# An order of its own for the first two images of a group-norm and attention kernel

## The reference

```python
g = group_norm(x, 32 groups, eps=1e-5)            # mean and variance over 6 channels x 1024 positions
qkv = einsum('bnc,oc->bno', g_tokens, qkv_w)      # 6 heads of 32
attn = softmax(einsum('bhnd,bhmd->bhnm', q, k) * 32**-0.5)
out = einsum('bhnm,bhmd->bhnd', attn, v)          # 1024 x 1024 per head
y = x + (out @ proj_w.T + proj_b)
```

## Time and profile before

| | us |
|---|---|
| median of 3 runs | 1629.27 |
| lowest, highest | 1627.18, 1630.30 |
| profiled execution, time | 1626.17 |
| profiled execution, span | 1624.4 |
| PE busy | 1502.3 (92%) |
| POOL busy | 1319.5 (81%) |
| ACT busy | 1197.5 (74%) |
| DVE busy | 1164.1 (72%) |

### The profile page before, as it was taken

One profiled execution on the slowest core, in us unless ns is written; L12 is line 12 of the kernel. 1 busy time (PEld: TensorE's weight loads), 2 busy tenths in 40 slices (PEclk: granted clock), 3 DMA queues, 4 the chain that ended last, 5 costly groups with the idle time before them and its releaser, 6 DMA issues.

```text
span 1624.4 us, 24488 instructions
## 1 busy us (share of the span) xinstructions
PE 1502.3 (92%) x8800; PEld 514.2 (32%) x8800; DVE 1164.1 (72%) x2022; ACT 1197.5 (74%) x2001; POOL 1319.5 (81%) x645
## 2 busy tenths in 40 slices
PE   3379999999999999999999999999999999999872
PEld 1123233333333333333333333333333333333210
DVE  3387868778787877877786877877787887877500
ACT  2138787877869787887978787887968787777750
POOL 4028898988989898998989898998989898888880
PEclk9989999999999999999999999999999999999985
DMA  2304051352616043251515144251615223141112
GB/s 73 59 27 86 22 94 39 78 88 54 106 41 116 24 103 57 63 102 54 105 41 105 28 94 72 57 108 35 117 37 100 45 76 64 54 86 37 30 46 59
DMA packets 86105, 108.86 MB, mean 67 GB/s; under 512 B 38240, under 2 KB 50912, under 8 KB 85984
## 3 DMA queue, kind: packets, MB, share of 16 engines
q1 hardware_dynamic: 85984, 107.30, 32.2%
HBM read 42.98 MB, written 13.15 MB: 35 GB/s over the span
## 4 chain that ended last, share of the span: by engine, by line
PE 62%; DMA 9%; ACT 8%; POOL 5%; SPq 5%; issue 2%; DVE 2%; POOLq 0%; DVEq 0%; ACTq 0%
PE heads_ps L561 16%; PE max_ps L470 14%; PE scores_ps L546 14%; DMA sums_spread<-sums_sb 7%; PE extra_ps L520 6%; ACT probs L675 4%; PE extra_ps L529 3%; SPq L351 3%; POOL prob_pairs L728 2%; POOL prob_pairs L734 2%; PE extra_ps L533 2%; PE extra_ps L531 2%; PE extra_ps L530 2%; PE extra_ps L534 2%; SPq L428 1%
## 5 line engine op out<-in xcount | busy, mean ns | idle before, releaser
L675 ACT ACTIVATE probs<-scores_ps,exp_scale 128x512 f32<-128x512 f32 x1536 | 974.8, 698 | 292.5 <-PE scores_ps L546 287.2
L829 DVE TENSOR_REDUCE half_max<-max_ps 128x1 f32<-128x512 f32 x1536 | 981.1, 682 | 290.2 <-PE max_ps L470 279.9
L728 POOL TENSOR_TENSOR prob_pairs<-probs 128x1024 f32<-128x1024 f32 x384 | 896.3, 2360 | 173.9 <-ACT probs L675 173.2
L470 PE MATMUL max_ps<-k_stack,q_stack 96*128 96x512 f16 x1536 | 588.1, 384 | 23.9 <-DVE half_max L829 14.8
L546 PE MATMUL scores_ps<-q_stack,k_stack 98*128 98x512 f16 x1536 | 581.7, 380 | 14.0 <-DMA q_stack<-shift_rows 8.1
L561 PE MATMUL heads_ps<-probs,v_sb 128*32 128x512 f32 x3072 | 410.7, 607 | 1.5 <-ACT probs L675 0.8
L470 PEld LDWEIGHTS max_ps<-k_stack,q_stack 96*128 96x128 f16 x1536 | 150.3, 98 | 297.5 <-issue 104.2
L734 POOL TENSOR_TENSOR prob_pairs<-prob_pairs 128x1024 f32<-128x1024 f32 x96 | 224.2, 2357 | 0.0
L546 PEld LDWEIGHTS scores_ps<-q_stack,k_stack 98*128 98x128 f16 x1536 | 150.2, 98 | 182.2 <-ACT probs L675 34.1
L520 PE MATMUL extra_ps<-prob_pairs,ones 128*32 128x512 f32 x1152 | 134.0, 598 | 5.8 <-POOL prob_pairs L728 5.8
L561 PEld LDWEIGHTS heads_ps<-probs,v_sb 128*32 128x32 f32 x3072 | 61.0, 108 | 152.4 <-issue 130.5
(11 more groups left out here) (82 smaller groups left out, 956.8 us busy)
## 6 DMA issues: line engine op xcount, KB each, us to landing
q_stack<-qk_hi SPq DMA_DIRECT2D x96, 128.0 KB, 4.2
k_stack<-qk_hi SPq DMA_DIRECT2D x96, 128.0 KB, 5.8
inv_sb<-inv_rows SPq DMA_DIRECT2D x48, 256.0 KB
x_res<-x SPq DMA_DIRECT2D x16, 768.0 KB, 5.4
out<-x_res SPq DMA_DIRECT2D x16, 768.0 KB, 4.8
x_sb<-x SPq DMA_DIRECT2D x16, 512.0 KB, 6.7
x_sb<-x SPq DMA_DIRECT2D x32, 256.0 KB, 8.0
q_stack<-qk_lo SPq DMA_DIRECT2D x48, 128.0 KB, 4.5
```

What stands on the lines that cost most here:

```text
L470: pe.matmul(max_ps[:, bank, :], q_stack[0:STACK, par, h, P * tile:P * (tile + 1)], k_stack[0:STACK, par, h, HALF * half:HALF * (half + 1)] ...
L675: nc.scalar.activation(probs[:, a, s % RING, HALF * half:HALF * (half + 1)], scores_ps[:, u_bank(s, u), :], ACT.Exp, scale=exp_scale[:, 0: ...
L728: nc.gpsimd.tensor_tensor(prob_pairs[:, a, q, :], probs[:, a, (s - 1) % RING, :], probs[:, a, s % RING, :], ALU.add).then_inc(pairs_added, 1)
L829: nc.vector.tensor_reduce(half_max[:, a, tile, half:half + 1], max_ps[:, bank, :], AX_X, ALU.max).then_inc(max_read[bank], 1)
```

## The change

It gives steps -2 and -1 their own lists of slots, and changes these things:

- The six qk products of image 0 go to six banks (`qk_bank`: extra_ps, heads_ps, the three scores banks, one max bank), and PE no longer waits for `extra_freed` between them. All later products go through extra_ps as before.
- SP stacks pair 0 of image 0 once four products are read, pair 1 and pair 2 once all six are; image 1's norm is written between pairs 0 and 1 and read between pairs 1 and 2.
- There are two x buffers (and two of `chan_norm`). Image 1 is loaded right behind the constants, image 2 in step -2 at slot 10, image 3 in step -1 at slot 23; from step 0 on, image b+4 at slot 10.
- Statistics of image 1 are taken by DVE during the weights' setup and aggregated behind it; its POOL operations come in slot 11 of step -2. From step -1 on, bn_stats of image b+3 stand in slots 8 to 11, one a slot, instead of two each in slots 16 and 17.
- In step -1 the value products are in slots 10, 13, 14, 15 (14, 15, 18, 20 before), the qk products of image 1 in 19, 21, 22 (17, 19, 22), the shift of pair 0 in slot 20 (21), ACT's normalisation of image 1 in slots 16 to 19 (3 to 9), POOL's low parts in 18 and 20 (8 and 10).
- In the last attending step the shifts are in slots 4 and 12 (5 and 13), whose move stands in SP's program before the heads' moves of slots 5 and 13.

```diff
-STATS_AT = ((16, 1), (16, 3), (17, 1), (17, 3))
+STATS_AT = ((8, 1), (9, 1), (10, 1), (11, 1))
...
-QK_SECOND_SLOTS = (17, 19, 22)
-V_SECOND_SLOTS = (14, 15, 18, 20)
+QK_SECOND_SLOTS = (19, 21, 22)
+V_SECOND_SLOTS = (10, 13, 14, 15)
+SHIFT_FIRST_SLOTS = {20: 0}
+SHIFT_LAST_SLOTS = {4: 1, 12: 2}
+XHAT_SECOND_AT = ((16, 1), (16, 3), (17, 1), (17, 3), (18, 1), (18, 3), (19, 1), (19, 3))
+XLO_SECOND_SLOTS = (18, 20)
+RSTD_SECOND_SLOT = 11
+STACK_FIRST_SLOTS = {16: 0, 18: 1, 20: 2}
+NORM_SECOND_SLOTS = (17, 19)
+LOAD_SECOND_SLOT = 23
...
-        self.take_stats = 0 <= at + 3 < BATCH
+        self.take_stats = -1 <= at < BATCH - 3
+        self.first, self.second = at == -2, at == -1
...
+        self.shift_slots = {-1: SHIFT_FIRST_SLOTS, BATCH - 1: SHIFT_LAST_SLOTS}.get(at, SHIFT_SLOTS)
...
-        x_sb = sb("x_sb", [P, 2, N], F32)
+        x_sb = sb("x_sb", [P, 2, 2, N], F32)
...
+        def qk_bank(st, i):
+
+            if not st.first or i == 0:
+                return extra_ps[:, :]
+            return heads_ps[:, :] if i == 1 else (scores_ps[:, i - 2, :] if i < 5 else max_ps[:, 0, :])
...
+            load_x(1)
...
+            write_stats(0)
+            read_stats(0)
+            write_norm(0)
+            write_stats(1)
+            read_norm(0)
+            read_stats(1)
...
+                    if st.first and s in STACK_FIRST_SLOTS:
 
                         sp.wait_ge(extra_freed, st.ordinal(s))
-                        for p in range(PAIRS):
-                            stack_pair(st.parity, p)
+                        stack_pair(st.parity, STACK_FIRST_SLOTS[s])
+                    if st.first and s == NORM_SECOND_SLOTS[0]:
+                        write_norm(1)
+                    if st.first and s == NORM_SECOND_SLOTS[1]:
+                        read_norm(1)
...
-                    if s == LOAD_SLOT and st.project_in and b + 3 < BATCH:
+                    if s == st.load_slot and -2 <= b < BATCH - 4:
                         sp.wait_ge(xhat_ready, XHAT * (b + 3))
-                        load_x(b + 3)
+                        load_x(b + 4)
...
-                if part == 0 and due(g):
+                if part == 0 and due(g) and not st.first:
                     pe.wait_ge(extra_freed, g)
...
-            statistics(-3)
+            statistics(0)
+            for n in range(2 * HALVES):
+                half_statistics(1, n)
             dve.wait_ge(l1_ready, 1)
...
+            statistics(1)
```

More of the change, by code:

```diff
@@ L127, in __init__ @@
         self.late = at >= 0 and self.follow
+        self.shift_slots = {-1: SHIFT_FIRST_SLOTS, BATCH - 1: SHIFT_LAST_SLOTS}.get(at, SHIFT_SLOTS)
+        self.xhat_at = XHAT_SECOND_AT if self.second else XHAT_AT
+        self.xlo_slots = XLO_SECOND_SLOTS if self.second else XLO_SLOTS
+        self.load_slot = LOAD_SECOND_SLOT if self.second else LOAD_SLOT
         self.extras = extras
     def extra(self, s):
-        if s in SHIFT_SLOTS and (self.follow if SHIFT_SLOTS[s] == 0 else self.attend):
-            return "shift", SHIFT_SLOTS[s]
+        if s in self.shift_slots and (self.follow if self.shift_slots[s] == 0 else self.attend):
+            return "shift", self.shift_slots[s]
         if self.follow and s in self.v_slots:
@@ L284, in group_norm_attention @@
         shift_set = sem("shift_set")
-        x_loaded = sem("x_loaded")
+        x_loaded = [sem(f"x_loaded{i}") for i in range(2)]
         stats_step = sem("stats_step")
@@ L356, in step @@
                 for s in range(SLOTS):
[L357 to L367, removed]
@@ L379, in step @@
-                    if s == QK_FIRST_SLOTS[-1] + 1 and not st.follow and st.project_in:
-                        sp.wait_ge(extra_freed, st.ordinal(s))
-                        for p in range(PAIRS):
-                            stack_pair(st.parity, p)
+                    if st.project_in and st.attend and s == NORM_OUT_SLOT:
+                        write_norm(b + 2)
+                    if st.project_in and st.attend and s == NORM_IN_SLOT:
+                        read_norm(b + 2)
+                    if st.take_stats and s == STATS_OUT_SLOT:
+                        write_stats(b + 3)
@@ L491, in fill @@
                     o, n = slice(P * t, P * (t + 1)), slice(HALF * half, HALF * (half + 1))
-                    last = product(part, extra_ps[:, :], w_hi[:, :, o], w_lo[:, :, o], xhat_a_hi[:, par, n],
+                    last = product(part, qk_bank(st, i), w_hi[:, :, o], w_lo[:, :, o], xhat_a_hi[:, par, n],
                                    xhat_a_lo[:, par, n], xhat_b[:, par, n])
@@ L872, in step @@
                             read(st, s - 1)
[L873 to L876 removed]
+                        if st.take_stats and (s, u) in STATS_AT:
+                            half_statistics(st.b + 3, STATS_AT.index((s, u)))
+                        if st.take_stats and (s, u) == AGGREGATE_AT:
+                            statistics(st.b + 3)
                         if st.maxed(s) is not None:
```

109 lines of the change are left out of this document (66 added, 43 removed).

## The result

| | before | after |
|---|---|---|
| median, us | 1629.00 (4 runs) | 1588.78 (4 runs) |
| lowest, highest | 1627.18, 1630.30 | 1587.34, 1589.81 |
| profiled execution, time and span | 1626.17, 1624.4 | 1588.74, 1586.9 |

The ratio is 0.9753, 95% interval 0.9736 to 0.9770. The medians differ by 40.2 us. The profiled spans differ by 37.5, because the execution profiled before was 2.8 under its own median. Forecast were 35.4 and 1594; the range, 1587 to 1604, holds the result.

What follows compares the result with a forecast made beforehand. PE fills the steady steps; the front is a relay of waits, DVE limiting its last part, and the end has score waits. Front 30.4, steady 0 and end 5 sum to 35.4 us: 1629.27 to 1594, range 1587 to 1604.

Steps and rivals of the forecast that it cites:

- Load of image 1: Start of the front: small statistics transfers queue behind image 1's load, adding 2.5 us from the aggregate on; bounds 0 and 4.5.
- Six banks: Front: no PE waits between image 0's six products; two take 2.1 us, four 1.07; all read by 42.2.
- Rival (a): Front: PE stays on the lower clock through the six products and restarts on it for the maxima; about 1598; chance 0.12.
- Stacks and first maximum: Front: pair 0's stacks start after four products, at 40.0, and take 7.1 us; first row maximum on DVE at 47.7.
- Image 1's small transfers: Front, between the stack pairs: each queues, the norm landing near 53; the aggregate's wait leaves the row maxima.
- rival (b): Front: image 1's norm queues behind the stacks, ACT normalises late and slots 19 to 23 stand; 1602; chance 0.11.
- Rival (d): Front keeps its length because some SP wait holds the stacks as late as before; 1624 or no gain; chance 0.04.
- Maxima until the first exponential: Step -1, slots 12 to 23: row maxima on DVE from 47.7, with 1.1 and 1.3 us added; first exponential at 81.8.
- Steady steps: Steps with bn_stats moved to slots 8 to 11: taken 0, between a gain of 9 us and an equal loss.
- Rival (c): Steady steps: bn_stats in slots 8 to 11 delay maxima that PE's queue waits on; about 1653, slower; chance 0.03.
- Last step: Last attending step: earlier shifts remove two score waits, 2.7 and 3.6 us, POOL nearly as late; 5 us gained, bounds 1 and 6.
- The signs: Right: first product near 32, exponential near 82; wrong: exponential after 90, or exponential-to-end differing over 8 us from 1512.

Runs made afterwards that it cites:

- the load moved: Changed kernel with image 1's load issued behind the read of image 0's norm, its bn_stats and aggregate behind the weights: 1585.62 us, ratio 0.9731.
- PE kept busy: Changed kernel plus PE matmuls in step -1 whose result nobody reads: 1589.20 us, ratio 0.9748 to the kernel before.
- one bank: Changed kernel with the six first products through one bank again, waiting for its release between them: 1597.69 us, ratio 0.9801.
- the reads behind the stacks: Changed kernel with image 1's statistics read, aggregated and its norm moved only behind the 18 stack transfers: 1600.91 us, ratio 0.982.
- the stacks together: Changed kernel with pair 0's stack transfers waiting for all six first products instead of four: 1592.83 us, ratio 0.9757.
- both loads moved: Changed kernel with image 1 loaded behind the read of image 0's norm and, from step 0 on, loads in slot 16: 1582.37 us, ratio 0.9695.

## Why the prediction was right, point by point

**Load of image 1.** Forecast 2.5 us at the aggregate; it came at 15.75 in place of 13.42, 2.3 us later, and with the load moved it was back at 13.16. Missing was a second effect: the norm's read took 1.0 us longer. The forecast had put what stands around it at nothing ("Nothing"). First product at 33.17, forecast 32.3.
The Trainium skill (DMA: Bandwidth & Descriptors, Queues, rings and completion order) has a queue's descriptors consumed in ring order on each DMA engine. By that rule the small transfers come behind those of the load, and the trace and the run with the load moved agree (2.3 and 2.6 us at the aggregate).

**Six banks.** Forecast: two products on the lower level, four at 1.07, all read by 42.2. Measured: the level rose inside the second, the rest follow at 1.08, all read at 42.58. Rival (a) was that the level stays low through all six: it did not. Choosing the two gap-free stretches of the earlier trace rows over the many rows of the front was right. The six banks by themselves are worth 8.4 us.

**Stacks and first maximum.** Forecast 47.7; measured 48.84. The first product was 0.9 late, and the stacks' transfers took 7.7 us from first issue (40.45) to PE (48.19), taken as 7.1.

**Image 1's small transfers.** Forecast: no wait. Right; rival (b) did not come. Putting the small transfers back in the old place costs 11.6 us of time; the forecast counted a DVE wait of 10 as removed. Rival (d), a front as long as before, fell with the first exponential at 83.31.

**Maxima until the first exponential.** Forecast 34.1 us (47.7 to 81.8), measured 34.5. Its two additions for the lower level and a late product, 1.1 and 1.3, compare with the 3.2 us that the kernel with PE kept busy saves here. Front in all: 28.9 in place of 30.4. The new slots of step -1 have no experiment of their own; that the 5.91 us wait is gone is shown by the trace alone.

**Step 0.** Taken as unchanged. It lost 1.5 us: PE enters it on the lower level. This term was not in the sum. That the next rise of the level could fall into step 0 was to be read from the earlier trace rows, where PE works on the lower level behind a wait. Kept busy, PE needs 85.7, 1.3 less than before. Without idle matmuls the level there differs from kernel to kernel: slots 0 and 1 take 2.4 and 3.3 us with one bank, with the reads behind the stacks, with the stacks together and with both loads moved, and 6.7 to 8.3 together in the others that start from the changed kernel. Up to 2.6 us of any difference between these kernels can be this.

**Steady steps.** This is the term that was mis-sized: "Taken: 0". Measured +4.8. The part that is shown is the projection's read in slot 18, 0.16 us a step, 1.9 over steps 1 to 12. The forecast counted DVE's busy share in the slots that receive bn_stats, and never looked at who waited in the slots that lose them. Another 2.2 us are in slot 14, where the earlier trace rows were rightly named as the place. But what set the wait was misread: "behind shifts and low parts". It was the shift's read behind a reciprocal, behind the transfer of the sums, behind the load of x. The load stays in slot 10 in the change, and kernels with the same steady program had from 49.5 to 54.2 us there, a range that holds the 51.9 of before. So these 2.2 us can be chance. Rival (c), bn_stats in slots 8 to 11 delaying maxima, did not come: slot 8 took 41.4 us over the twelve steps, 41.9 before.

**Last step.** Forecast 5 (1 to 6), measured 5.9 in the trace and 6.0 by undoing it. POOL was nearly as late, and followed: two of its three pauses went. The middle one kept 2.08 of 2.44, where 0.9 less was forecast.

**Sum.** Off by -1.5 in the front, -1.5 in step 0, +4.8 in the steady steps, +0.9 and -0.5 at the end: +2.1 on the profiled spans, and 2.7 more between the medians, because the profiled execution of before was a fast one. That the result lies within the range is in part luck. It is 1.8 us over the low end, and that end was built from no queueing, no added DVE waits and an end of 6, with nothing for a gain in the steady steps. Had the front and step 0 come as forecast, the same steady steps would have put the time some 3 us lower, just outside.

**The signs.** One sign of being wrong did come: a stretch from the first exponential to the end that differs by over 8 us from 1512. It was 1503.6 us (83.31 to 1586.9), 8.6 less than the 1512.2 of before. The sign was set too tight, since the forecast itself moved that stretch by its 5 us at the end, but it does point at the term that was wrong, the steady steps. The signs of being right came, but for the middle one of POOL's pauses.

## What to carry to other kernels

Where an engine's program waits for a small transfer, look for what is issued ahead of that transfer on the same queue, and move the bulk load to where nobody waits: that gave 4.6 us in the steady steps and 3.7 at the start. When work moves between slots, look at the slots that it leaves as well as at those that receive it. An edit that shows its effect in the trace and none in the time (here, matmuls that hold the clock up) is worth a second try on top of the next fix: the same edit came with 0 us the first time and 4.3 the second.

## What the runs showed of the hardware

- In the stretch of the row maxima, with PE busy 28.9 of 36 us (48 to 84), the granted clock was 0.78, and it was 0.50 at 84.00 to 86.60, where PE was busy all the time. With 46 matmuls more, 30 of them one a unit, it read 1.00 in both stretches.
- Durations tell more than the clock column. The column reads 1.00 for 33.5 to 42.6 us of the changed kernel, while the matmuls from 33.17 to 35.68 take the lower level's 0.58 to 0.63 us.
- The level rose 2.9 us after the first of the six gap-free products (33.17 to 36.10). In another execution of a kernel with the same products it was later: the second product's copy came 2.13 us behind the first's (36.21, 38.34) in place of 1.45.
- The read of image 0's norm took 3.1 us to ACT before, and 4.1 with image 1's load and its statistics' write issued ahead of it. It took 4.2 with nothing read behind it, and 3.0 to 3.2 with load and write both behind it. Which of the two costs the 1.0 was not tried.
